# Reordering the state part of a fused Mamba and expert-FFN kernel: B copied first, state product and state step moved forward

## The chip, the cores and the metric

The kernel runs on one core of a Trainium2 chip. The metric is the device time of one execution in microseconds (us), the median of several runs. The engines are named as in the profile: PE (TensorE; PEld is its weight load), DVE (VectorE), ACT (ScalarE), POOL (GpSimd) and SP (SyncE, which here only issues DMAs).

## The reference, cut to what matters

The input x is 8 sequences of 1024 tokens by 256 features. One layer is a mixer with a residual, then a feed-forward part with a residual:

```python
x = x + layernorm(u + mamba(rmsnorm(u)))      # u = layernorm(x)
x = x + layernorm(ffn(layernorm(x)))          # dense MLP + 1024 experts, top 8 of 64x(16..64) keys, 4 heads
```

The mixer works in chunks of 128 tokens, with 8 heads of 64 features and a state of 128 per head. In one chunk, after a projection, a causal convolution over 4 taps and a silu:

```python
scores  = (C @ B.T) * decay * dt              # within the chunk
Y_intra = scores @ X
S       = (B * w).T @ X                       # what the chunk adds to the state
Y_inter = (C * exp(cum)) @ H                  # what the state before gives to the chunk
H       = exp(cum_last) * H + S               # the state step
y = rmsnorm((Y_intra + Y_inter + D*X) * silu(z)) @ out_w
```

## The kernel before, in words

Work is cut into 32 groups of 256 tokens, and a group into two chunks c = 0, 1. Each engine runs its own instruction list, written out by hand in a function `do_group(g, e, f, n)`; a hardware loop runs it once per period. In one period four groups are in flight: group g is in the mixer, e = g-1 in the first half of the feed-forward part, f = g-2 in its last part, and n = g+1 only has its input normalised. Engines execute their lists strictly in order, and semaphores order them against each other (`X.at(g, k)` is the count that says step k of group g is done). So the order of calls in each engine's `do_group` is the schedule.

PSUM is eight banks: `ring[0:2]` (the projection's pairs, X transposed, the state products), `pairb[0:2]` (decay rows, B transposed, scores, y transposed, the output), `yb` (hT, cum, the intra-chunk output), `f0` (the feed-forward output) and `products` (two banks, the expert products).

First part of a period. PE computes ten pairs of projection tiles (`mixer_pair`, L1340) into `ring`, with the feed-forward matmuls of e and f between them. ACT takes the halo and begins each pair (`mixer_pair`, L685 and L694), DVE adds three taps (`mixer_conv`, L998 and L1008), ACT applies silu (L675). DVE's top-8 search `ffn_best(e, c)` (L1097 on) stands between conv(6), conv(7) and conv(8, 9).

Second part, the state part. PE, in this order: `mixer_X(g, 0)` (L1391), the transposes of W (L1534), the expert products (L1504), the decay rows (`mixer_rows`, L1376 and L1379), `ffn_out(f, 1)` (L1554), `mixer_hT(n)` (L1309), B transposed (`mixer_B`, L1400), scores (L1423), the inter-chunk product `mixer_Yi` (L1413), the intra-chunk product `mixer_Yn` (L1448 and L1452), then for chunk 1 X and rows, the state product of chunk 0 `mixer_S` (L1432), B, scores, Yi, Yn, y transposed (`mixer_yT`, L1461), `mixer_S` of chunk 1, and the output matmuls (`mixer_out`, L1471). The next period's first pair (L1340) stands right behind.

ACT copies what PE transposes: `mixer_B` is `Btok` (L741), which scores waits for; `mixer_hT` is L659, `mixer_move` is `Xt` (L734), `mixer_decay` is `Ldec` (L723, four instructions of a half), `ffn_out` is `f` (L843). `mixer_square(g, c)` (L757) squares the gated y for the norm and waits for DVE's `mixer_gate(g, c)`. DVE multiplies scores by decay (`mixer_scores`, `sL`, L1024), scales Yi by exp(cum) (`mixer_state`, L1034), adds Yn and gates by z (`mixer_gate`, L1045 and L1048), adds S to H (`mixer_step`, L1040), and between these works through the experts of e (`ffn_last` L1159, `ffn_mask` L1168, `ffn_times` L1177) and stores f (`ffn_store`, L1191 and L1195). The period ends on DVE with `tail_sum` (L1059), which waits for the output matmuls. POOL scales X (L467, L473, L493), builds the expert scores (`weigh`, L535), scales the state (`mixer_decay`, L484), and makes the small roots (L508 and L510, `rsf`).

Of the kernel before, what the change touches and what calls it, by code (L numbers as in the profile page):

```python
# [73 lines left out]
def sandwich(nc, x, in_wT, norm_w, conv_w, conv_b, dt_bias, A_log, D_skip, gnorm_w, out_wT,  # L74
# [21 lines left out]
    with ExitStack() as ctx:  # L96
# [227 lines left out]
        def _(pool):  # L324
# [233 lines left out]
            def do_group(g, e, f, n):  # L558
                a, b, c = g is not None, e is not None, f is not None
                if a:  # L560
                    mixer_dt_abs(g)
                if b:
                    tail_root4(e)
                if c:
                    collect(f, 0, 2, 3)
                if a:
                    mixer_dt(g)
                    mixer_keep(g)
                if c:
                    collect(f, 1, 1, 2, 3)  # L570
                if a:
                    mixer_cum(g)
                if n is not None:
                    mixer_norm(n)
                    mixer_halo(n)
                if a:
                    mixer_scale(g, 0)
                    mixer_skip(g, 0)
                if b:
                    weigh(e, 0, 0, 1, 2, 3)  # L580
                if a:
                    mixer_decay(g, 0)
                if c:
                    tail_root(f, statsf, mvf, vf, rsf, rootf)
                if a:
                    mixer_scale(g, 1)
                    mixer_skip(g, 1)
                    mixer_decay(g, 1)
                if b:
                    weigh(e, 1, 0, 1)  # L590
                if a:
                    mixer_root_y(g)
                if b:
                    collect(e, 0, 1)
                if a:
                    tail_root(g, stats3, mv2, ve3, rs3, root3)
                if b:
                    weigh(e, 1, 2, 3)
                pool.wait_ge(own_pool, own.n)
                pool.sem_clear(own_pool)  # L600
                own.restart()
# [14 lines left out]
        def _(act):  # L616
# [228 lines left out]
            def do_group(g, e, f, n):  # L845
                a, b, c = g is not None, e is not None, f is not None

                def pairs(*js):

                    for j in js:  # L850
                        if a:
                            if j >= 2:
                                silu(g, j - 2)
                            mixer_pair(g, j)

                pairs(0, 1)
                if a:
                    mixer_dt(g)
                pairs(2)
                if a:  # L860
                    mixer_u(g)
                if b:
                    tail_norm(e, g)
                pairs(3)
                if b:
                    tail_h2T(e)
                if a:
                    mixer_dt_exp(g)
                    mixer_z(g, 0)
                    mixer_z(g, 1)  # L870
                if b:
                    ffn_sim(e, 0)
                if c:
                    ffn_experts(f, 1, 0)
                pairs(4)
                if b:
                    ffn_sim(e, 1)
                if c:
                    ffn_experts(f, 1, 1)
                pairs(5)  # L880
                if c:
                    ffn_experts(f, 1, 2)
                if b:
                    ffn_up(e, 0)
                if c:
                    ffn_WT(f, 0)
                pairs(6)
                if c:
                    ffn_experts(f, 1, 3)
                if b:  # L890
                    ffn_up(e, 1)
                pairs(7)
                if a:
                    mixer_cum(g)
                pairs(8)
                if b:
                    ffn_up(e, 2)
                pairs(9)
                if b:
                    ffn_up(e, 3)  # L900
                if a:
                    silu(g, PAIRS - 2)
                    silu(g, PAIRS - 1)
                    mixer_move(g, 0)
                if c:
                    ffn_WT(f, 1)
                if b:
                    ffn_exp(e)
                if a:
                    mixer_exp(g)  # L910
                    mixer_decay(g, 0)
                if n is not None:
                    mixer_norm(n, e)
                    mixer_hT(n)
                if c:
                    ffn_out(f)
                if a:
                    mixer_B(g, 0)
                if a:
                    mixer_move(g, 1)  # L920
                    mixer_decay(g, 1)
                    mixer_square(g, 0)
                    mixer_B(g, 1)
                if b:
                    tail_keep(e)
                    ffn_experts(e, 0, 0, 1)
                if a:
                    mixer_yT(g, 0)
                    mixer_square(g, 1)
                    mixer_yT(g, 1)  # L930
                if b:
                    ffn_experts(e, 0, 2)
                if b:
                    ffn_experts(e, 0, 3)
# [14 lines left out]
        def _(dve):  # L949
# [87 lines left out]
            def mixer_step(g, c):  # L1037
                dve.wait_ge(H_scaled.sem, H_scaled.at(g, c))
                dve.wait_ge(S_ps.sem, S_ps.at(g, c))
                V.tensor_tensor(H[:], H[:], ring[c][:], ALU.add).then_inc(H_done.sem, 1)  # L1040
# [156 lines left out]
            def do_group(g, e, f, n):  # L1197
                a, b, c = g is not None, e is not None, f is not None

                def conv(*js):  # L1200
                    for j in js:
                        if a:
                            mixer_conv(g, j)

                conv(0)
                if b:
                    tail_residual(e)
                conv(1)
                if c:
                    ffn_last(f, 1)  # L1210
                    ffn_mask(f, 1, 0)
                conv(2, 3)
                if c:
                    ffn_times(f, 1, 0)
                    for h in range(1, RH):
                        ffn_mask(f, 1, h)
                        ffn_times(f, 1, h)
                conv(4, 5, 6)
                if b:
                    ffn_best(e, 0)  # L1220
                conv(7)
                if b:
                    ffn_best(e, 1)
                conv(8, 9)
                if n is not None:
                    mixer_stats(n)
                if b:
                    ffn_choose(e)
                if c:
                    ffn_stats(f)  # L1230
                if a:
                    mixer_scores(g, 0)
                    mixer_state(g, 0)
                if b:
                    ffn_last(e, 0)
                    ffn_mask(e, 0, 0)
                if c:
                    ffn_store(f)
                if a:
                    mixer_gate(g, 0)  # L1240
                    mixer_step(g, 0)
                if b:
                    ffn_times(e, 0, 0)
                    ffn_mask(e, 0, 1)
                if a:
                    mixer_scores(g, 1)
                if b:
                    ffn_times(e, 0, 1)
                if a:
                    mixer_state(g, 1)  # L1250
                if b:
                    ffn_mask(e, 0, 2)
                if a:
                    mixer_gate(g, 1)
                if b:
                    ffn_times(e, 0, 2)
                if a:
                    mixer_step(g, 1)
                if b:
                    ffn_mask(e, 0, 3)  # L1260
                    ffn_times(e, 0, 3)
                if a:
                    tail_sum(g)
                dve.wait_ge(own_dve, own.n)
                dve.sem_clear(own_dve)
                own.restart()
# [19 lines left out]
        def _(pe):  # L1286
# [271 lines left out]
            def do_group(g, e, f, n):  # L1558
# [54 lines left out]
                    mixer_rows(g, 0, f)  # L1613
                if c:
                    ffn_out(f, 1)
                if n is not None:
                    mixer_hT(n, e)
                if a:
                    mixer_B(g, 0)
                    mixer_scores(g, 0)  # L1620
                    mixer_Yi(g, 0)
                    mixer_Yn(g, 0, e, n)
                    mixer_X(g, 1)
                    mixer_rows(g, 1, f)
                    mixer_S(g, 0)
                    mixer_B(g, 1)
                    mixer_scores(g, 1)
                    mixer_Yi(g, 1)
# [66 lines left out]
```

## Time and profile before

| what | us |
|---|---|
| median of 3 runs | 3009.18 |
| lowest and highest | 2999.34 and 3031.3 |
| the profiled execution's own time | 3042.37 |
| its span, first to last instruction | 3040.6 |
| PE busy | 2806.7 (92%) |
| DVE busy | 2522.2 (83%) |
| POOL busy | 2016.2 (66%) |
| ACT busy | 1722.3 (57%) |
| mean granted TensorE clock | 0.963 |

The last row says what share of full speed the chip granted to PE, averaged over the span; 1.00 is 2.4 GHz and 0.50 is 1.2 GHz. Times of day in the rows are us from the span's start. A group of instructions in the trace carries its count (x16), the time from its first start to its last end, and in brackets the idle time of its engine before it, with what ended it.

### The profile page before, as it was taken

Reading aid. Unit: us, or ns where it says so; the run is one execution under the profiler, and the core shown is the slowest. Engines: PE = TensorE matmul, PEld = TensorE weight load, DVE = VectorE, ACT = ScalarE, POOL = GpSimd, SP = SyncE. Lnnn points to the kernel's source line nnn. Section 1 sums busy time; section 2 is a strip of 40 time slices with the busy share of each in tenths; the row PEclk is TensorE's granted clock in tenths of the full one; section 3 lists DMA queues with packets and bytes.
Section 4 is the critical chain, followed back from the end, with each engine's and each line's share of the span. In section 5 each row is a group of like instructions: output and inputs, shape, how many; then the busy total and the mean of one; then the engine's idle time right before and its main releaser. Section 6 shows DMA issues by size and latency. Waiting matters only on the chain.

```text
span 3040.6 us, 50162 instructions
## 1 busy us (share of the span) xinstructions
PE 2806.7 (92%) x14784; PEld 2295.6 (75%) x14784; DVE 2522.2 (83%) x6406; ACT 1722.3 (57%) x3560; POOL 2016.2 (66%) x2388
## 2 busy tenths in 40 slices
PE   5899999999999999999999999999999999999985
PEld 4777777777777777877777777777777777777763
DVE  4588888888888888888888888888888888888874
ACT  4465556655665655556655565555566555556542
POOL 3287667676677676667676667676667676676755
PEclk9999999999999999999999999999999999999997
DMA  3000000000000000000000000000000000000000
GB/s 124 8 8 11 8 7 7 10 10 10 7 7 10 7 10 10 10 3 7 10 10 10 3 10 7 10 10 10 3 10 7 10 10 10 3 10 7 8 4 7
DMA packets 28183, 34.24 MB, mean 11 GB/s; under 512 B 2672, under 2 KB 27248, under 8 KB 27440
## 3 DMA queue, kind: packets, MB, share of 16 engines
q1 hardware_dynamic: 28144, 33.77, 3.4%
q8 instruction: 19, 0.31, 0.0%
q14 instruction: 20, 0.16, 0.0%
HBM read 25.37 MB, written 8.39 MB: 11 GB/s over the span
## 4 chain that ended last, share of the span: by engine, by line
PE 43%; DVE 23%; ACT 13%; POOL 10%; issue 9%; ACTq 1%; DMA 0%; DVEq 0%; SPq 0%; POOLq 0%
DVE acc L1008 9%; PE bank L1340 8%; POOL Em L535 7%; PE bank L1546 7%; PE bank L1471 4%; PE bank L1359 4%; PE products L1504 4%; PE bank L1423 3%; PE bank L1413 3%; ACT Em L824 2%; ACT WT L834 2%; DVE s L1097 2%; PE bank L1452 2%; PE bank L1495 2%; PE bank L1432 2%
## 5 line engine op out<-in xcount | busy, mean ns | idle before, releaser
L1008 DVE SCALAR_TENSOR_TENSOR acc<-bank,cw,acc 128x253 f32<-128x253 f32 (+2 forms) x1920 | 774.3, 473 | 0.0
L1340 PE MATMUL bank<-hT,w_in 128*128 128x256 f32 x2560 | 608.5, 383 | 11.6 <-DVE acc L1008 10.9
L1340 PEld LDWEIGHTS bank<-hT,w_in 128*128 128x128 f32 x2560 | 485.0, 192 | 117.8 <-issue 44.4
L535 POOL TENSOR_TENSOR Em<-ee 128x1024 f32<-128x1024 f32 x256 | 519.4, 2054 | 28.7 <-issue 28.7
L1168 DVE SCALAR_TENSOR_TENSOR Em<-Em,p 128x1024 f32<-128x1024 f32 x256 | 371.5, 1451 | 0.0
L550 POOL TENSOR_TENSOR W<-W,Em 128x1024 f32<-128x1024 f32 x128 | 335.9, 2624 | 8.6 <-ACT Em L824 0.3
L824 ACT ACTIVATE Em<-Em,rden 128x1024 f32<-128x1024 f32 x256 | 292.5, 1143 | 64.6 <-DVE Em L1177 63.0
L694 ACT ACTIVATE acc<-bank,cb,cw 128x256 f32<-128x256 f32 x640 | 325.2, 561 | 0.0
L1177 DVE TENSOR_TENSOR Em<-Em,products 128x1024 f32<-128x1024 f32 x256 | 311.0, 1215 | 4.5
L675 ACT ACTIVATE xbcT<-acc 128x512 f32<-128x512 f32 x320 | 200.6, 627 | 102.5 <-DVE acc L1008 102.2
L1504 PE MATMUL products<-w_de,h2T 128*128 128x512 f32 x512 | 235.4, 603 | 23.0 <-DVE Em L1177 23.0
L1423 PE MATMUL bank<-xbcT 128*128 128x128 f32 x1024 | 161.1, 322 | 100.5 <-ACT Btok L741 100.5
L1519 PE MATMUL bank<-h2T,w_up 128*128 128x256 f32 x1024 | 242.2, 380 | 1.4 <-ACT sim L796 0.7
L1554 PE MATMUL bank<-w_ue,WT 128*128 128x256 f32 x1024 | 233.8, 382 | 2.1 <-ACT WT L834 2.1
L359 POOL TENSOR_SCALAR ve<-mv 128x2 f32<-128x2 f32 x32 | 9.0, 280 | 341.0 <-DVE mv L976 341.0
L1546 PE MATMUL bank<-w_down,hid 128*128 128x256 f32 x1024 | 233.8, 382 | 0.0
L1423 PEld LDWEIGHTS bank<-xbcT 128*128 128x128 f32 x1024 | 146.2, 228 | 115.7 <-ACT Btok L741 115.7
L1519 PEld LDWEIGHTS bank<-h2T,w_up 128*128 128x128 f32 x1024 | 194.7, 190 | 28.6 <-ACT sim L796 1.5
L1546 PEld LDWEIGHTS bank<-w_down,hid 128*128 128x128 f32 x1024 | 194.2, 192 | 28.6 <-issue 0.7
L1554 PEld LDWEIGHTS bank<-w_ue,WT 128*128 128x128 f32 x1024 | 193.8, 192 | 28.1 <-ACT WT L834 2.5
L685 ACT ACTIVATE halo<-bank 128x6 f32<-128x6 f32 x320 | 56.0, 175 | 273.2 <-PE bank L1340 273.1
L484 POOL TENSOR_TENSOR H<-H,ecum 128x512 f32<-128x512 f32 x64 | 66.7, 1042 | 201.6 <-PE bank L1413 201.6
(177 smaller groups left out, 5799.8 us busy)
## 6 DMA issues: line engine op xcount, KB each, us to landing
x_in<-x_dram SPq DMA_DIRECT2D x32, 256.0 KB, 2.7
x_res<-x_dram SPq DMA_DIRECT2D x32, 256.0 KB, 2.6
out_dram<-f SPq DMA_DIRECT2D x32, 256.0 KB, 2.2
w_in<-in_wT_dram SPq DMA_DIRECT2D x1, 3080.0 KB, 13.0
w_up<-upT_dram SPq DMA_DIRECT2D x1, 1024.0 KB, 15.7
w_de<-down_eT_dram SPq DMA_DIRECT2D x1, 1024.0 KB, 17.7
w_down<-downT_dram SPq DMA_DIRECT2D x1, 1024.0 KB, 19.7
w_ue<-up_e_dram SPq DMA_DIRECT2D x1, 1024.0 KB, 21.8
```

The source lines that it names most:

```text
L535: nc.gpsimd.tensor_tensor(Em[:, k], bc(ee[:, k, 0:XD], 2, KEYS), bc(ee[:, k, XD:XD + KEYS], 1, XD), ALU.mult).then_inc(E_done.sem, 1)
L550: nc.gpsimd.tensor_tensor(W[:], flat[0] if h == 1 else W[:], flat[h], ALU.add)\
L694: last = nc.scalar.activation(acc[:, r, a], ps[:, a * TOK:(a + 1) * TOK], ACT.Identity, scale=cw[:, t, TAPS - 1:TAPS], bias=cb[:, t:t + 1])
L824: nc.scalar.activation(flat, flat, ACT.Silu, scale=rden[:, c, h:h + 1]).then_inc(Zs_done.sem, 1)
L1008: ins = V.scalar_tensor_tensor(acc[:, r, a, ahead:], ps[:, a * TOK:(a + 1) * TOK - ahead], cw[:, t, k:k + 1], acc[:, r, a, ahead:], ALU.mu ...
L1168: V.scalar_tensor_tensor(flat, flat, p8[:, k, TOP - 1:TOP], flat, ALU.is_ge, ALU.mult)\
L1340: last = mm(ring[j % 2][:, a * TOK:(a + 1) * TOK], w_in[:, k, at:at + P], hT[:, k, :], start=k == 0, stop=k == DK - 1)
L1423: last = mm(pairb[q][:, i * P:(i + 1) * P], xbcT[:, INNER // P + h, c * P:(c + 1) * P], xbcT[:, INNER // P + HEADS + h, c * P:(c + 1) * P] ...
L1504: last = mm(fA[:, q * 512:(q + 1) * 512], h2T[:, k, c * P:(c + 1) * P], w_de[:, k, q * 512:(q + 1) * 512], start=k == 0, stop=k == DK - 1)
L1519: last = mm(yb[:, a * TOK:(a + 1) * TOK], w_up[:, k, (2 * j + a) * P:(2 * j + a + 1) * P], h2T[:, k, :], start=k == 0, stop=k == DK - 1)
L1546: last = mm(f0[:, c * D:(c + 1) * D], hid[:, i, c * P:(c + 1) * P], w_down[:, i, :], start=False, stop=False)
L1554: last = mm(f0[:, c * D:(c + 1) * D], WT[:, 4 * q + i, :], w_ue[:, 4 * q + i, :], start=False, stop=c == CH - 1 and q == 1 and i == 3)
```

## The change

Only the order of calls changes, on all four compute engines. POOL scales the state (`mixer_decay(g, 0)`) after the first expert head instead of after the fourth. ACT copies B of chunk 0 ahead of `ffn_out` and `mixer_hT`, and B of chunk 1 ahead of the square. DVE runs conv(8) ahead of the second `ffn_best`, `mixer_state` ahead of `mixer_scores`, and `mixer_step` ahead of `ffn_store` and `mixer_gate`. PE runs B and Yi of chunk 0 ahead of `mixer_hT`, and S ahead of Yn.

```diff
 POOL
-                    weigh(e, 0, 0, 1, 2, 3)
+                    weigh(e, 0, 0)
                 if a:
                     mixer_decay(g, 0)
+                if b:
+                    weigh(e, 0, 1, 2, 3)
 ACT
                     mixer_norm(n, e)
+                if a:
+                    mixer_B(g, 0)
+                if c:
+                    ffn_out(f)
+                if n is not None:
                     mixer_hT(n)
-                if c:
-                    ffn_out(f)
-                if a:
-                    mixer_B(g, 0)
                 if a:
                     mixer_move(g, 1)
                     mixer_decay(g, 1)
+                    mixer_B(g, 1)
                     mixer_square(g, 0)
-                    mixer_B(g, 1)
 DVE
-                conv(7)
+                conv(7, 8)
                 if b:
                     ffn_best(e, 1)
-                conv(8, 9)
+                conv(9)
...
                 if a:
+                    mixer_state(g, 0)
                     mixer_scores(g, 0)
-                    mixer_state(g, 0)
                 if b:
                     ffn_last(e, 0)
                     ffn_mask(e, 0, 0)
+                if a:
+                    mixer_step(g, 0)
                 if c:
                     ffn_store(f)
                 if a:
                     mixer_gate(g, 0)
-                    mixer_step(g, 0)
 PE
+                if a:
+                    mixer_B(g, 0)
+                    mixer_Yi(g, 0)
                 if n is not None:
                     mixer_hT(n, e)
                 if a:
-                    mixer_B(g, 0)
                     mixer_scores(g, 0)
-                    mixer_Yi(g, 0)
+                    mixer_S(g, 0)
                     mixer_Yn(g, 0, e, n)
                     mixer_X(g, 1)
                     mixer_rows(g, 1, f)
-                    mixer_S(g, 0)
                     mixer_B(g, 1)
```

## Rows read from the trace of the kernel before

**Rows 1.** The page: PE's share of the span, and the chain that ended last.

```profile
PE 2806.7 (92%) x14784; PEld 2295.6 (75%) x14784; DVE 2522.2 (83%) x6406; ACT 1722.3 (57%) x3560; POOL 2016.2 (66%) x2388
...
PE 43%; DVE 23%; ACT 13%; POOL 10%; issue 9%; ACTq 1%; DMA 0%; DVEq 0%; SPq 0%; POOLq 0%
```

**Rows 2.** Stretches of one period: length, busy PE PEld DVE ACT POOL, clock, DMA, GB/s.

```profile
913.53:1002.63 89.10, 84.31 (x463) 68.97 (x462) 77.93 (x200) 53.53 (x111) 63.34 (x75) 1.00 0.03 9
1278.01:1371.56 93.55, 88.77 (x463) 72.86 (x462) 78.97 (x201) 52.82 (x111) 63.07 (x75) 0.95 0.03 8
```

**Rows 3.** Timeline of DVE: L1059 of the third and of the last period.

```profile
275.71 0.88 DVE L1059 SCALAR_TENSOR_TENSOR v<-bank,rsy,u 128x256 f32<-128x256 f32 x2 [1.20 <-PE bank L1471]
...
2934.70 0.88 DVE L1059 SCALAR_TENSOR_TENSOR v<-bank,rsy,u 128x256 f32<-128x256 f32 x2 [1.56 <-PE bank L1471]
```

**Rows 4.** Timeline of PE, state part of one period at full clock.

```profile
966.64 0.38 PE L1376 MATMUL bank<-mask_b,ident_b 128*128 128x512 bf16 x1
...
974.57 2.05 PE L1423 MATMUL bank<-xbcT 128*128 128x128 f32 x16 [0.79 <-ACT Btok L741]
...
980.84 0.61 PE L1391 MATMUL bank<-ident,xbcT 128*128 128x128 f32 x4
...
983.49 1.90 PE L1432 MATMUL bank<-Xw,Btok 128*128 128x64 f32 x16
...
988.86 2.05 PE L1423 MATMUL bank<-xbcT 128*128 128x128 f32 x16 [2.59 <-ACT Btok L741]
990.75 1.90 PE L1413 MATMUL bank<-H,xbcT 128*128 128x64 f32 x16
...
993.39 1.89 PE L1452 MATMUL bank<-Xdt,sL 128*128 128x64 f32 x16
...
1000.46 1.97 PE L1471 MATMUL bank<-w_out,yT 128*128 128x256 f32 x8 [0.78 <-ACT yT L765]
1002.26 3.62 PE L1340 MATMUL bank<-hT,w_in 128*128 128x256 f32 x16
```

**Rows 5.** Timeline of PE, the same product in a period with a lower clock.

```profile
1172.68 3.52 PE L1413 MATMUL bank<-H,xbcT 128*128 128x64 f32 x16
```

**Rows 6.** Stretches of that period: PE waiting, then PE behind the wait.

```profile
1167.80:1170.20 2.40, 0.00 (x0) 0.00 (x0) 2.37 (x4) 1.24 (x4) 2.02 (x2) 1.00 0.30 109
...
1172.00:1178.00 6.00, 6.00 (x25) 4.97 (x23) 4.04 (x5) 3.02 (x5) 1.64 (x2) 0.50 0.00 0
```

**Rows 7.** Timeline of DVE in the full-clock period.

```profile
956.10 1.11 DVE L1097 MAX8 s<-sim 128x8 f32<-128x64 f32 x8
...
980.96 2.06 DVE L1168 SCALAR_TENSOR_TENSOR Em<-Em,p 128x1024 f32<-128x1024 f32 x1
983.94 1.45 DVE L1191 TENSOR_SCALAR f<-f,mvf,rsf 128x256 f32<-128x256 f32 x2 [0.92 <-POOL rsf L510]
...
987.49 0.67 DVE L1040 TENSOR_TENSOR H<-H,bank 128x512 f32<-128x512 f32 x1
...
989.22 1.27 DVE L1168 SCALAR_TENSOR_TENSOR Em<-Em,p 128x1024 f32<-128x1024 f32 x1
990.41 1.28 DVE L1024 TENSOR_TENSOR sL<-bank,Ldec 128x512 f32<-128x512 f32 x2
...
995.40 0.69 DVE L1045 TENSOR_TENSOR yv<-yv,bank 128x512 f32<-128x512 f32 x1 [0.46 <-PE bank L1452]
...
1000.21 1.22 DVE L1177 TENSOR_TENSOR Em<-Em,products 128x1024 f32<-128x1024 f32 x1
```

**Rows 8.** Timeline of ACT in the full-clock period.

```profile
956.14 1.01 ACT L694 ACTIVATE acc<-bank,cb,cw 128x256 f32<-128x256 f32 x2
...
982.59 2.25 ACT L723 ACTIVATE Ldec<-bank,ncum 128x128 f32<-128x128 f32 x8 [0.51 <-PE bank L1379]
...
988.23 1.06 ACT L741 ACTIVATE Btok<-bank 128x512 f32<-128x512 f32 x2
```

**Rows 9.** Timeline of POOL in the full-clock period.

```profile
992.82 1.04 POOL L484 TENSOR_TENSOR H<-H,ecum 128x512 f32<-128x512 f32 x1 [4.35 <-PE bank L1413]
```

More of the change, by code:

```diff
@@ L913, in do_group @@
                     mixer_norm(n, e)
-                    mixer_hT(n)
+                if a:
+                    mixer_B(g, 0)
                 if c:
                     ffn_out(f)
-                if a:
-                    mixer_B(g, 0)
+                if n is not None:
+                    mixer_hT(n)
                 if a:
```

## The prediction

> **What bounds the kernel now.** I read the page first. PE is busy for 92% of the span, DVE for 83%, and the chain that ended last lies on PE for 43%, on DVE for 23%, on ACT for 13% and on POOL for 10% [rows 1]. So no engine alone sets the time: a period starts with a PE-bound stretch, and then a chain that crosses all four engines decides when the output matmuls are done and the next period's first pair may start.
>
> Next I measured the period, from one L1059 to the next. From the third to the last there are 29 periods in 2934.70 - 275.71 = 2658.99 us [rows 3], a mean of 91.69. But single periods differ: 89.10 at a granted clock of 1.00, 93.55 at 0.95 [rows 2]. Three periods in a row, ending with the one shown, are the 89.1 kind. The work is the same, so this trace holds its own experiment: 29 x 89.10 = 2583.9, and the remaining 75.1 us, 2.6 per period, are what the lower clock costs. The stretches of one slowed period show where it happens: PE does nothing for 2.40 us at clock 1.00, and from 1172 to 1178 it is granted 0.50, which is 1.2 GHz instead of 2.4 [rows 6]; the inter-chunk product takes 3.52 us there against 1.90 at full clock [rows 4, 5]. What PE did before the fall is wait for Btok, 2.59 us in the period shown [rows 4]. That longest wait of the period does not bring the fall every time (this very period kept its clock), but falls come after it.
>
> Why that wait: ACT copies B of chunk 1 behind the square of chunk 0, at 988.23 [rows 8], the square waits for DVE's gate, the gate for the store of f, and the store for POOL's rsf (0.92 idle ahead of it) [rows 7].
>
> **The change part by part**, on the full-clock period. Nothing is added or removed; no DMA moves.
>
> *conv(8) ahead of the second top-8 search.* DVE is free at 956.10 [rows 7], but ACT has only just begun pair 8: L694 starts at 956.14 and takes 1.01 [rows 8]. Today the search fills this time. With the new order DVE idles about 1.05 us plus a hand-over that I estimate at 0.15 from the other places where conv waits for ACT: 1.2 us. Conv(9) ends 1.2 later, so do the silu, X's copy, WT's copy, the exponentials, the expert choice, POOL's four expert heads, rsf, and the store. PE gains nothing from the earlier conv(8): its products then end sooner, and it waits for WT's copy instead, so that the decay rows start some 0.46 later than 966.64 [rows 4] (1.2 less 0.75 of slack between that copy's first half and the rows). Bounds: 0, if DVE arrives late anyway, and 1.4, if the hand-over is twice as long. I take +1.2 on the DVE and POOL chain.
>
> *B and Yi of chunk 0 first, hT and ffn_out behind.* This fills the 0.79 wait for Btok at 974.57 [rows 4]: 1.7 us of Yi stand in it. The copies of f and hT come about 1 us later on ACT, which waits afterwards anyway for X of chunk 1. f's statistics are then ready near 976, and POOL wants them only near 983. Cost 0.
>
> *S ahead of Yn.* PE's S at 983.49 takes 1.90 from first start to last end, of which some 0.16 lies under the next operation: 1.74 [rows 4]. It moves in front of X of chunk 1, which then starts at 980.84 + 0.46 - 0.79 + 1.74 = 982.25. Rows follow, and Ldec starts 982.59 + 1.4 = 984.0 and ends at 986.25 [rows 8]. Formerly S hid the wait for Ldec; now PE waits about 1.2 us there in three pieces (under each half of B, and for the first half of Btok).
>
> *POOL's state decay after one head, DVE's step ahead of the store.* Four heads plus decay take POOL the same time in either order; Yi is ready near 975.6 and POOL asks near 976.5, so nothing stalls. DVE has its step ready near 982.4, behind the mask, and waits for rsf until 985.1 (983.9 + 1.2): the step is free there, and its 0.67, or 0.60 without what overlaps its neighbour, leaves the tight part [rows 7]. mixer_state ahead of scores likewise uses time in which DVE waits: 0.
>
> *B of chunk 1 copied ahead of the square.* Btok starts at 986.25, behind Ldec, instead of 988.23 [rows 8]. Scores start near 986.9 instead of 988.86, Yi ends near 990.2 instead of 992.48. Now sL is late: DVE reaches it at 990.41 + 1.2 - 0.6 = 991.0 and has it at 992.3 [rows 7]. The intra-chunk product starts at 992.4 instead of 993.39 [rows 4], so 0.99 earlier, after a wait of about 1.2. From there PE's list is unchanged down to the next first pair: 1002.26 - 1.0 = 1001.3. The gate no longer waits its 0.46 [rows 7].
>
> *Sum.* DVE's last product ends at 1000.21 + 1.22 + 1.2 - 0.6 - 0.46 = 1001.6; PE's outputs arrive at about the same time (formerly DVE waited 1.20 there) [rows 3]. So both chains give 1.0 us less, a full-clock period of 88.1. DVE is the bound of the second half then.
>
> *The clock.* PE's longest wait, 2.59, is split: 1.2 in three pieces around B, 1.2 ahead of Yn. In before, the other waits of 0.79 and 0.78 [rows 4] are followed by no fall. I take it that the falls go. Lower bound of this gain 0, upper 75.1 us. The Trainium skill (TensorE: Matmul & The Clock Gate, What's actually happening) says that the clock is gated by how busy PE has recently been; the halved clock behind PE's wait agrees [rows 6]. Leaving that page out changes no number here.
>
> Price of overlap: the mask takes 1.27 with POOL quiet (989.22) and 2.06 beside POOL's heads (980.96) [rows 7]. POOL's second decay moves from 992.82 [rows 9] to about 990.5, with two more heads behind it, so more of DVE's tight part lies beside POOL. Between 0 and 0.8 per period; I take 0.1, as the operations beside it are mostly the same in number. The Trainium skill (SBUF — State Buffer, Who interferes with whom) has an exclusive lock here for a DVE instruction with two SBUF inputs against POOL's reads. By its rule a mask caught behind a head could wait much of it; the rows show 0.79 more.
>
> Total: 2583.9 + 75.1 goes to 29 x 88.1 = 2554.9, that is -104; two more periods ahead of them at -1 each, and 0.1 x 31 back: about -103. The profiled execution's own 3042.4 becomes 2939. The median of before is 33 lower than this execution, presumably with fewer falls; a kernel with no falls should not share in that, so I leave 2939.
>
> **The rivals.**
> *A. The clock keeps falling as before,* 2.6 per period: the waits of 1.2 and 1.2 lie within 7 us, with transposes and short products between them. For it: the fall isn't strictly tied to the long wait. Against: the total idle near it falls from 2.6 to 1.2 at B. Time 2939 + 75 = 3014, no change against the median.
> *B. Slower: the stall ahead of conv(8) is passed through whole.* The DVE and POOL chain from conv(9) to the gate is the true bound, PE's earlier start only waits for it, and the clock still falls. Price 1.2 x 31 = 37: 3042 + 37 = 3079. It is slower by over 1% from 3039 on, so if the step and the gate's wait give back under 1.1 per period and the clock nothing. For it: rsf is waited for in every period. Against: 0.60 and 0.46 are plainly in the rows.
> *C. The stall costs nothing,* because DVE comes late to conv(8) anyway, behind a later tail_sum: then 31 x 1.2 less, 2902.
> *D. It doesn't do what it says:* Btok still comes late, since the Ldec ahead of it is slower or the second half of B waits. Then the clock falls in some periods: 2939 + 35 = 2975.
>
> **How the numbers follow.** The forecast has 0.60 (2915 to 2965), C 0.08, D 0.12, A 0.14, B 0.06. About 1% is what a measurement of this kernel can tell from no change: faster below 2979, slower above 3039. Faster: 0.60 + 0.08 + most of D, with a part of A: 0.79. Slower 0.06, same 0.15. The range goes from C to A, 2895 to 3012.
>
> **What the profile after would show.** Right: periods near 88, clock 1.00 in nearly all, Btok of chunk 1 ahead of the square, no PE wait over 1.5 us, L998 of pair 8 waiting about 1.2 for ACT, and L1452 waiting for sL (DVE) in chunk 1; the step ahead of the store with the wait for rsf shrunk. Wrong: stretches at 0.50 in the state part (A), or an Ldec that ends over 1 us later than 986.25 relative to its period (D), or periods over 91 at clock 1.00 (B).

## The result, and the profile after

The changed kernel takes 3118.38 us (median of 4, 3114.32 to 3120.07), against 3019.44 for the kernel before (median of 4: the three runs above and one more): a ratio of 1.0318, with a 95% interval of 1.0263 to 1.0372. It is slower. The forecast was 2939 with a range from 2895 to 3012, so both the direction and the range were wrong. The profiled execution has a span of 3118.3. Each later experiment had the kernel before measured beside it, at 3023.66, 3028.17 or 3029.76, and its ratio is to that; so differences of a few us between experiments mean nothing.

Three lines of the page of the changed kernel; its line numbers are up to 4 above those of before:

```profile
span 3118.3 us, 50134 instructions
...
PE 2865.9 (92%) x14784; PEld 2337.5 (75%) x14784; DVE 2581.2 (83%) x6406; ACT 1724.7 (55%) x3560; POOL 1965.3 (63%) x2388
...
PE 63%; DVE 16%; POOL 9%; issue 7%; ACT 4%; DMA 0%; DVEq 0%; ACTq 0%; SPq 0%; POOLq 0%
```

The same instructions are busy 59 us longer on PE and 59 us longer on DVE than before, and PE's share of the chain rose from 43% [rows 1] to 63%. The engines do no more work, they do it more slowly. Stretches of the changed kernel (length, busy time of PE, PEld, DVE, ACT, POOL, granted clock, DMA): two periods, then two pieces of the second one.

```profile
1135.02:1228.19 93.17, 87.81 (x463) 71.85 (x462) 80.67 (x200) 53.67 (x111) 61.32 (x74) 0.96 0.03 8
1228.19:1323.01 94.82, 89.47 (x463) 73.18 (x462) 79.86 (x200) 53.59 (x111) 61.32 (x74) 0.95 0.03 8
1306.10:1308.70 2.60, 0.00 (x0) 0.00 (x0) 2.60 (x4) 2.57 (x5) 2.60 (x2) 1.00 0.00 0
1310.00:1317.00 7.00, 7.00 (x33) 6.82 (x33) 5.35 (x7) 2.24 (x4) 3.51 (x4) 0.50 0.00 0
```

These answer to [rows 2] and [rows 6]. No period of the loop keeps full clock any more. Before, 3 of the 29 did. Over the 29 periods the granted clock stood at 0.50 for 270 us, and before for 167. PE still waits in one piece, 2.6 us, and its clock is still 1.2 GHz behind it; only the place is new. PE's timeline in that period, against [rows 4]:

```profile
1281.89 0.39 PE L1380 MATMUL bank<-mask_b,ident_b 128*128 128x512 bf16 x1 [1.27 <-ACT WT L836]
...
1290.62 1.95 PE L1427 MATMUL bank<-xbcT 128*128 128x128 f32 x16
...
1303.22 1.90 PE L1417 MATMUL bank<-H,xbcT 128*128 128x64 f32 x16
1304.95 1.08 PE L1452 MATMUL bank<-DX,ident 128*128 128x512 f32 x2
1308.76 3.21 PE L1456 MATMUL bank<-Xdt,sL 128*128 128x64 f32 x16 [2.73 <-DVE sL L1027]
...
1312.61 3.52 PE L1436 MATMUL bank<-Xw,Btok 128*128 128x64 f32 x16
1315.91 3.71 PE L1475 MATMUL bank<-w_out,yT 128*128 128x256 f32 x8
...
1322.64 3.62 PE L1344 MATMUL bank<-hT,w_in 128*128 128x256 f32 x16
```

```profile
1300.66 0.62 ACT L743 ACTIVATE Btok<-bank 128x512 f32<-128x512 f32 x1
```

The wait for Btok in chunk 0 is gone, and B's copy for chunk 1 (the ACT row) and the second Yi come early, as forecast. Then PE waits 2.73 for sL, where I had 1.2, and the intra-chunk product, S and the output matmuls run at half speed (3.71 for the output against 1.97 in [rows 4]). Why sL is late stands on DVE and POOL, side by side in time:

```profile
1271.93 0.35 DVE L1001 SCALAR_TENSOR_TENSOR acc<-bank,cw,halo_sum 128x3 f32<-128x3 f32 x2 [1.07 <-ACT acc L696]
...
1296.92 0.68 DVE L1043 TENSOR_TENSOR H<-H,bank 128x512 f32<-128x512 f32 x1
1299.90 2.25 DVE L1194 TENSOR_SCALAR f<-f,mvf,rsf 128x256 f32<-128x256 f32 x2 [2.31 <-POOL rsf L510]
1302.19 1.41 DVE L1198 TENSOR_TENSOR f<-f,x_late 128x512 f32<-128x512 f32 x1
...
1305.97 1.43 DVE L1171 SCALAR_TENSOR_TENSOR Em<-Em,p 128x1024 f32<-128x1024 f32 x1
1307.33 1.27 DVE L1027 TENSOR_TENSOR sL<-bank,Ldec 128x512 f32<-128x512 f32 x2
```

```profile
1299.84 1.04 POOL L467 TENSOR_TENSOR Xdt<-Xt,dts 128x512 f32<-128x512 f32 x1
1300.96 1.04 POOL L473 TENSOR_TENSOR Xw<-Xdt,ecum 128x512 f32<-128x512 f32 x1
1301.96 1.09 POOL L493 TENSOR_TENSOR DX<-Xt,head_c 128x512 f32<-128x512 f32 x1
```

The store of f took 1.45 in its first part before [rows 7] and 0.69 in its second (L1195, 22.2 us over 32 in its group). It now takes 2.25 + 1.41, together 1.5 more. Beside it POOL runs three operations back to back. Before, the second of them waited for S of chunk 0 (23.8 us in 32 waits), which PE computed late; S is early now, so this gap in POOL's list is gone, and with it the room in which DVE worked undisturbed.

The chain that ended last shows it piece by piece. Rows are start, length and what was running; "issue" is a wait for nothing that the profile shows:

```profile
1299.90 0.03 DVE f L1194
1299.94 1.01 issue
1300.95 1.21 DVE f L1194
1302.19 0.03 DVE f L1198
1302.22 0.09 issue
1302.33 1.20 issue
1303.53 0.69 DVE yv L1048
```

The second half of L1194 gets going at 1300.95, when POOL's first operation has ended (1299.84 + 1.04 = 1300.88). Until then DVE's first half is on record as running, for 1.13 us; but it took 1.13 before the change as well, since POOL's first operation lay beside it there too. New are the second half of L1194, 1.20 instead of 0.40, with POOL's second operation beside it, and L1198, 1.41 instead of 0.69, beside the third.

### The profile page after: what moved, and what is told of

It reads as the page before. It is cut to its first block, busy times and chain, and to the rows that moved or that the text cites. A ratio compares the mean times of both kernels' runs of the same rounds, so it can differ in the third digit from the quotient of the medians.

```text
span 3118.3 us, 50134 instructions
## 1 busy us (share of the span) xinstructions
PE 2865.9 (92%) x14784; PEld 2337.5 (75%) x14784; DVE 2581.2 (83%) x6406; ACT 1724.7 (55%) x3560; POOL 1965.3 (63%) x2388
## 4 chain that ended last, share of the span: by engine, by line
PE 63%; DVE 16%; POOL 9%; issue 7%; ACT 4%; DMA 0%; DVEq 0%; ACTq 0%; SPq 0%; POOLq 0%
PE bank L1344 16%; PE bank L1558 7%; PE bank L1550 7%; POOL Em L535 7%; PE bank L1475 5%; DVE acc L1011 5%; PE bank L1523 4%; PE bank L1363 4%; PE products L1508 4%; PE bank L1499 4%; PE bank L1436 3%; PE bank L1456 3%; PE bank L1383 2%; DVE Em L1171 2%; DVE Em L1180 1%
## 5 line engine op out<-in xcount | busy, mean ns | idle before, releaser
L535 POOL TENSOR_TENSOR Em<-ee 128x1024 f32<-128x1024 f32 x256 | 544.0, 2145 | 28.5 <-issue 28.5
L1171 DVE SCALAR_TENSOR_TENSOR Em<-Em,p 128x1024 f32<-128x1024 f32 x256 | 448.5, 1752 | 0.0
L1456 PEld LDWEIGHTS bank<-Xdt,sL 128*128 128x128 f32 x1024 | 141.3, 217 | 122.0 <-issue 122.0
L1456 PE MATMUL bank<-Xdt,sL 128*128 128x64 f32 x1024 | 144.0, 302 | 81.8 <-DVE sL L1027 81.8
L1001 DVE SCALAR_TENSOR_TENSOR acc<-bank,cw,halo_sum 128x3 f32<-128x3 f32 x640 | 109.5, 212 | 119.4 <-ACT acc L696 119.3
```

The costliest lines, as they stand in the source:

```text
L535: nc.gpsimd.tensor_tensor(Em[:, k], bc(ee[:, k, 0:XD], 2, KEYS), bc(ee[:, k, XD:XD + KEYS], 1, XD), ALU.mult).then_inc(E_done.sem, 1)
L1171: V.scalar_tensor_tensor(flat, flat, p8[:, k, TOP - 1:TOP], flat, ALU.is_ge, ALU.mult)\
L1456: last = mm(yb[:, h * HD:(h + 1) * HD], sL[:, h, :], Xdt[:, h * HD:(h + 1) * HD], start=False, stop=h == HEADS - 1)
```

## The experiments

Two things are suspected, the granted clock and the store of f, and the parts of the change may differ in sign. A kernel that keeps PE busy in its wait measures the order alone, at full clock.

**PE kept busy in its wait, both orders.** The same addition in both; in the old order ahead of the second scores, in the new one ahead of the intra-chunk product of chunk 1:

```diff
+            def warm(f, count):
+                if f is not None:
+                    pe.wait_ge(f_sb.sem, f_sb.at(f))
+                    for _ in range(count):
+                        mm(f0[:], zero_b[:], mask_b[:].rearrange("p h t -> p (h t)"), start=True, stop=True)
...
                     mixer_B(g, 1)
+                    warm(f, 11)
                     mixer_scores(g, 1)
```

Old order:

> The order of before, with eleven 128x512 bf16 matmuls of zeros on PE (some 2.4 us) in its 2.59 us wait ahead of the scores of chunk 1; they go to the bank f0, which holds nothing then, and change no result. Theory 1 (the clock falls because PE has been idle there): no stretch at 0.50 is left in the loop and every period takes 89.1 to 89.4 us, so the profiled execution comes to 3040 - 75 = 2965 (2955 to 2985). Theory 2 (the falls have another cause, the short products around the wait for instance): the mean period stays near 91.5 and the time near 3020.

New order:

> The changed kernel, with eleven such matmuls in the 2.73 us wait for sL ahead of the intra-chunk product of chunk 1. Theory 1 (most of the 2.6 us per period that the change cost is the clock, which now stays at 0.50 longer and over dense output matmuls): periods near 90.0 at clock 1.00, and 3118 - 31 x 3.9 = 2997 (2980 to 3015), still some 25 above the old order treated alike, since DVE reaches sL 1.6 us later than I forecast. Theory 2 (the new order is slow by itself, and the clock is beside the point): over 3060. Theory 3 (my forecast of the order was right at full clock): periods of 88.1, 2940.

Measured: 2960.68 (ratio to before 0.9817, 0.9734 to 0.9901) and 2985.78 (0.9897, 0.9867 to 0.9928). One period of each:

```profile
1251.86:1340.86 89.00, 86.38 (x469) 69.87 (x472) 77.83 (x201) 53.52 (x111) 63.23 (x75) 1.00 0.03 9
```

```profile
1355.32:1445.20 89.88, 86.52 (x470) 69.89 (x473) 79.04 (x201) 53.71 (x112) 62.24 (x75) 1.00 0.03 9
```

Work that computes nothing makes both kernels faster: the falls come from PE's idleness in those waits. It also divides the result, roughly, since the medians of before alone lie 10 us apart. At full clock the new order costs 2985.8 - 2960.7 = 25 us. The clock costs the old order 3019.4 - 2960.7 = 59 us, and the new one 3118.4 - 2985.8 = 133, which is about half of its 270 us at 0.50. Of the 99 us by which the change is slower, some 74 are the clock.

**Conv(8) alone, and taken back.**

```diff
-                conv(7)
+                conv(7, 8)
                 if b:
                     ffn_best(e, 1)
-                conv(8, 9)
+                conv(9)
```

> The order of before with conv(8) ahead of the second top-8 search and nothing else. If the stall of 1.2 us that this puts on DVE is passed through whole: 3019 + 31 x 1.2 = 3056. If it is absorbed, because PE's wait for Btok is longer or the clock's falls differ: 3019 to 3030. If the clock's falls grow with the longer wait ahead of the scores: up to 3100.

> The changed kernel with conv(8) behind the second top-8 search again. The DVE chain to sL of chunk 1 is then 1.2 us shorter and PE's wait ahead of the intra-chunk product near 1.5 us. If the falls come from that wait: hardly any are left, and the period is 89 us, 2960 to 2990. If only the 1.2 us come back: 3118 - 37 = 3081. If contention of POOL and DVE in the state part is all that matters: 3100 and more.

> The order of before with only conv(8) moved, and sixteen matmuls of zeros (3.5 us) in PE's wait for Btok of chunk 1, which is 3.76 in that order. If the 132 us that conv(8) alone cost are 1.2 us of stall per period and the rest the clock: periods of 90.3 at clock 1.00, 2961 + 37 = 2998 (2990 to 3006). If the move costs more by itself: 3020 and more. If nothing but the clock: 2961.

Conv(8) alone: 3155.32 (1.0459, 1.0369 to 1.0549), with one other the dearest of all. Its price is not the 37 us of the stall but 132. PE's wait for Btok grew from 2.59 to 3.76, and the products behind it are slow:

```profile
1314.59 3.78 PE L1423 MATMUL bank<-xbcT 128*128 128x128 f32 x16 [3.76 <-ACT Btok L741]
1318.16 3.51 PE L1413 MATMUL bank<-H,xbcT 128*128 128x64 f32 x16
```

With PE kept busy it takes 3027.62 (1.0022, 0.9994 to 1.0050), 67 above the old order treated alike (2960.7) instead of the 37 expected: a mean period of 91.1 against 89.05, which is 2.0 more, not 1.2. So about half of the 132 is the later chain itself, and the other half the clock. The missing part stands in the store of f again, whose second operation had taken 0.69:

```profile
1444.10 1.45 DVE L1191 TENSOR_SCALAR f<-f,mvf,rsf 128x256 f32<-128x256 f32 x2 [0.92 <-POOL rsf L510]
1445.58 1.54 DVE L1195 TENSOR_TENSOR f<-f,x_late 128x512 f32<-128x512 f32 x1
```

Here DVE comes later relative to PE's S, POOL's gap is smaller (it waited 0.46 for S), and Xw runs beside the second operation. Taking conv(8) back from the changed kernel gives 3087.30 (1.0252, 1.0157 to 1.0347), 31 less. My third alternative was 3100 and more, my second 3081; it lies at the second. PE's wait for sL stays 2.73 in 24 of 29 periods, since both of its sides come earlier, and the clock falls in 27 of 29. Its two periods without a fall take 88.8, so even at full clock conv(8) cost about 1 us of each period.

**The other parts alone.** S, decay and step early:

```diff
-                    weigh(e, 0, 0, 1, 2, 3)
+                    weigh(e, 0, 0)
                 if a:
                     mixer_decay(g, 0)
+                if b:
+                    weigh(e, 0, 1, 2, 3)
...
+                    mixer_S(g, 0)
                     mixer_Yn(g, 0, e, n)
                     mixer_X(g, 1)
                     mixer_rows(g, 1, f)
-                    mixer_S(g, 0)
...
+                if a:
+                    mixer_step(g, 0)
                 if c:
                     ffn_store(f)
                 if a:
                     mixer_gate(g, 0)
-                    mixer_step(g, 0)
```

> The order of before with S of chunk 0 ahead of the intra-chunk product, POOL's decay after one head and DVE's step ahead of the store, nothing else. S no longer keeps POOL waiting, so the store of f is stretched by 1.5 us as in the changed kernel, the square and the Btok behind it come later, and PE's wait for Btok grows from 2.59 to about 3.5. Theory 1 (longer wait, longer falls): three windows at half clock per period, a period of 94 to 96, 3100 to 3160. Theory 2 (the step early gives back what the stretch takes, and the clock doesn't follow the wait): 3020 to 3050.

Measured 3157.34 (1.0443, 1.0393 to 1.0492). The size fits the first theory, but its mechanism doesn't. PE waits 6.27 for Btok, not 3.5, and the falls are hardly longer: 198 us at 0.50 over the 29 periods against 167 before, worth some 15 us, while the mean period grew from 91.69 to 95.55, which is 112 us over the same 29. The rest is the wait itself. The longest of this kernel's waits tells where it comes from:

```profile
POOL H L484 <- PE bank L1416: 373.9, 64, 9.4
```

POOL waits for Yi 64 times, twice per group, and 373.9 us in all; before it was 201.6 in 33. Without the chunk 0 part Yi comes late, POOL stands still after its first head, and rsf comes 3.3 us later in its period. In the changed kernel, which has that part, POOL waits for Yi only 75.2 us in 34 waits. So this part needs the next one.

Chunk 0 alone (B and Yi ahead of hT on PE, B's copy first on ACT, state first on DVE; PE's part is shown):

```diff
+                    mixer_B(g, 0)
+                    mixer_Yi(g, 0)
                     mixer_hT(n, e)
-                    mixer_B(g, 0)
                     mixer_scores(g, 0)
-                    mixer_Yi(g, 0)
```

> The order of before with only the chunk 0 part: B and the inter-chunk product ahead of hT, state ahead of scores. It takes 0.79 us off PE's wait ahead of the first scores, but nothing off the chain through POOL and DVE that ends in the square and in Btok of chunk 1. Theory 1 (what PE gains it waits for later, in one piece, and the clock falls for longer): the wait for Btok is about 3.4, periods are 92.5 to 95, 3060 to 3130. Theory 2 (the time of PE's earlier start is kept): 3019 - 31 x 0.8 = 2995. Theory 3 (neutral, and the clock doesn't follow): 3019.

Measured 3052.63 (1.0091, 1.0062 to 1.0121), against 3028.17 of before. PE's earlier start is not kept, as the first theory says, but the clock does not fall for longer: it stands at 0.50 for 113 us over the 29 periods, against 167 before. What makes this kernel slower is, by its rows, the store of f, which is stretched here too. S comes early, POOL no longer waits for it, and the store's operations take 1153 ns (mean of its first two) and 1366, against 792 and 693: 1.4 us more per period. With PE's earlier start this also makes PE's wait longer than the 3.4 that I gave:

```profile
1368.07 3.60 PE L1424 MATMUL bank<-xbcT 128*128 128x128 f32 x16 [4.96 <-ACT Btok L741]
```

A wait of 4.96 with a mean clock of 0.971, and one of 3.76 with 0.944 in the kernel with conv(8) alone: the length of the wait alone does not give the length of the fall.

B of chunk 1 ahead of the square, alone:

```diff
                     mixer_decay(g, 1)
+                    mixer_B(g, 1)
                     mixer_square(g, 0)
-                    mixer_B(g, 1)
```

> The order of before with one exchange: ACT copies B of chunk 1 ahead of the square of chunk 0. PE's 2.59 us wait for Btok goes, and sL (DVE, 1.6 us later) leaves a wait of some 0.3 to 1.0 ahead of the intra-chunk product. Theory 1 (falls follow the long wait): no falls, a period of 87.6 to 88.2, and 2910 to 2935, under both kernels. Theory 2 (the order of the state part has falls whatever its waits): 2975 to 3010.

Measured 2930.03 (0.9682, 0.9635 to 0.9729), as the first theory has it. This exchange is worth 98 us by itself, of which 2960.7 - 2930.0 = 31 would be there at full clock too, and it is one of the changed kernel's. PE's waits are short (0.51 for sL here, 0.63 or 0.64 in the other 28 periods), and no period of the loop has a fall:

```profile
1318.44 2.05 PE L1423 MATMUL bank<-xbcT 128*128 128x128 f32 x16 [0.25 <-ACT Btok L741]
...
1323.65 1.97 PE L1452 MATMUL bank<-Xdt,sL 128*128 128x64 f32 x16 [0.51 <-DVE sL L1024]
```

**POOL held until f is stored.** This is the test of the stretched store:

```diff
                     tail_root(f, statsf, mvf, vf, rsf, rootf)
+                    if a:
+                        pool.wait_ge(o_done.sem, o_done.at(f))
                 if a:
                     mixer_scale(g, 1)
```

It goes into the changed kernel:

> The changed kernel; before POOL scales X of chunk 1 it waits until DVE has stored f. In the changed kernel DVE's store took 2.25 + 1.41 us beside these three POOL operations, against 1.45 + 0.69 before. Theory 1 (the store is stretched by POOL's operations, this makes sL late, and the wait of PE ahead of the intra-chunk product, now 2.73, brings the falls): the store is back at 1.5 + 0.7, the wait shrinks to 1.3 to 1.8, few or no falls are left, the period goes to 88.5 to 89.5 and the time to 2940 to 2980. Theory 2 (the falls come from something other than that wait, and only the stretch itself is gained): 3118 - 31 x 1.3 = 3078. Theory 3 (the stretch has another cause): 3110 to 3130.

Measured 3013.73 (0.9959, 0.9935 to 0.9983). One added wait takes 105 us off and the loss against before is gone. The store is even shorter than before the change, 0.74 + 0.69:

```profile
1343.05 0.74 DVE L1196 TENSOR_SCALAR f<-f,mvf,rsf 128x256 f32<-128x256 f32 x2 [2.31 <-POOL rsf L510]
1343.83 0.69 DVE L1200 TENSOR_TENSOR f<-f,x_late 128x512 f32<-128x512 f32 x1
```

Its cause is shown by that: the same DVE operations, with only POOL's order against them changed. But it is not as fast as I expected, since the clock still falls in 16 of the 29 periods, right behind a wait of only 1.19. PE's longest wait in this kernel is another one, 1.49 ahead of the decay rows and 25 us earlier, where it waits for WT's copy; conv(8) makes it.

```profile
1439.79 1.97 PE L1458 MATMUL bank<-Xdt,sL 128*128 128x64 f32 x16 [1.19 <-DVE sL L1029]
...
1442.18 3.52 PE L1438 MATMUL bank<-Xw,Btok 128*128 128x64 f32 x16
```

The two kinds of period of this kernel:

```profile
1271.36:1360.46 89.10, 84.83 (x462) 69.20 (x464) 78.70 (x200) 52.51 (x110) 61.16 (x74) 1.00 0.03 9
1360.46:1452.41 91.95, 87.33 (x458) 71.35 (x460) 79.22 (x201) 54.65 (x112) 63.41 (x75) 0.96 0.03 9
```

The first kind shows that the store is not all. At full clock, and with a store shorter than before the change, this order takes 89.10, just what the old one took, and not the 88.1 of the forecast. DVE's list ends the period (no idle time ahead of L1064), and in it the masks are stretched; POOL's decay of chunk 1 and two heads now lie beside them. Before, the two masks around sL took 1.27 (989.22, in [rows 7]) and 1.60:

```profile
993.34 1.60 DVE L1168 SCALAR_TENSOR_TENSOR Em<-Em,p 128x1024 f32<-128x1024 f32 x1
```

In this kernel:

```profile
1347.41 1.93 DVE L1173 SCALAR_TENSOR_TENSOR Em<-Em,p 128x1024 f32<-128x1024 f32 x1
1348.44 1.80 POOL L484 TENSOR_TENSOR H<-H,ecum 128x512 f32<-128x512 f32 x1 [0.18 <-PE bank L1419]
1350.20 3.76 POOL L535 TENSOR_TENSOR Em<-ee 128x1024 f32<-128x1024 f32 x2
1352.19 2.85 DVE L1173 SCALAR_TENSOR_TENSOR Em<-Em,p 128x1024 f32<-128x1024 f32 x1
1360.46 0.87 DVE L1064 SCALAR_TENSOR_TENSOR v<-bank,rsy,u 128x256 f32<-128x256 f32 x2
```

They take 1.93 and 2.85. The mean of all masks, eight per period, is 1770 ns here and 1752 in the changed kernel, against 1451 before.

With conv(8) back as well, and then with five matmuls of zeros more ahead of the intra-chunk product:

> The changed kernel with conv(8) back and with POOL's wait for the store of f. At full clock 89.1 (the period of the kernel with POOL's wait) - 1.1 = 88.0. Theory 1 (falls depend on how long PE waits in one piece): its wait ahead of the intra-chunk product stays 1.2, as both sides of it move together, and falls remain in some periods: 2930 to 2980. Theory 2 (the falls of the kernel with POOL's wait came from the longer wait ahead of the decay rows that conv(8) makes): no falls, 2923.

> The kernel of the run before this one, with five matmuls of zeros in the 1.2 us ahead of the intra-chunk product. All theories: no falls, periods near 88.0, 2918 to 2928. It is the new order without its two costs, and tells what the order itself is worth: 2961 - 2923, 38 us, if the idea behind the steps of my sum is right.

Measured 2925.39 (0.9691, 0.9620 to 0.9762) and 2921.70 (0.9676, 0.9605 to 0.9746). There are no falls without the zeros either. PE's wait for sL is 0.73 to 1.10 there (mostly 0.82), not the 1.2 I gave, and the wait for WT's copy is gone; conv(8) was part of what kept falls alive, and which of the two waits mattered is not separated. Freed of these two costs the new order is 2960.7 - 2921.7 = 39 us faster than the old one at full clock. But not all of that is the order: B of chunk 1 first gives 31 of it alone, and POOL's wait helps the old order too, as the next kernel shows.

**The best found**, the old order with B of chunk 1 first and POOL's wait:

> Only B of chunk 1 ahead of the square, and POOL's wait for the store of f. If the stretch of the store (792 against 460 ns for each half) is on the path that ends in sL, which PE waits 0.51 us for: 88.2 - 0.5 = 87.7 and 2915. If POOL's later X of chunk 1 makes the intra-chunk product wait instead: 2930 to 2960.

Measured 2909.32 (0.9633, 0.9563 to 0.9703): 120 us below before (3029.76 beside it) and 209 below the changed kernel. POOL's wait is worth 2930.0 - 2909.3 = 21 here, 6 more than expected, and the masks take 1429 ns in the mean, the least of all these kernels. The other state parts of the change, which the kernel at 2921.7 has on top of this one, cost 12 us.

```profile
1321.49:1408.86 87.37, 84.40 (x459) 68.76 (x461) 77.93 (x202) 53.70 (x111) 62.55 (x75) 1.00 0.03 9
```

The 29 periods of the loop in the profiled executions, side by side. The last column is how long the granted clock stood at 0.50 in them, read from the clock of each period:

| kernel | median, us | mean period | us at 0.50 |
|---|---|---|---|
| before (profiled at 3042) | 3019 to 3030 | 91.69 | 167 |
| changed | 3118 | 94.21 | 270 |
| changed, conv(8) back | 3087 | 93.36 | 266 |
| changed, POOL waits | 3014 | 90.63 | 109 |
| conv(8) alone | 3155 | 95.46 | 290 |
| S, decay and step early | 3157 | 95.55 | 198 |
| chunk 0 alone | 3053 | 92.16 | 113 |
| all others | 2909 to 3028 | 87.3 to 91.1 | 0 |

## Why the prediction was wrong, step by step

At full clock the changed kernel takes 2985.8 where 2939 was forecast, 47 more, and the clock costs another 133. To compare places in a period I set the first part's last projection pair equal, 957.59 in the full-clock period of before and 1272.26 after: 314.67 apart.

*The stall ahead of conv(8)*: right on DVE, 1.07 idle and sL's chain about 1.2 later. Rsf was put at 985.1 and came at 1299.86 - 314.67 = 985.2. That PE gains nothing and waits for WT's copy is right too (1.27).

*B and Yi first, S early, decay and step early*: the step was to be free near 982.4 and ran at 1296.92 - 314.67 = 982.3. Btok was put at 986.25 and came at 1300.66 - 314.67 = 986.0, and the second Yi was to end near 990.2, and what stands behind it began at 1304.95 - 314.67 = 990.3. This geometry held to 0.3 us.

*Price of overlap* is the first step that failed. I took 0.1 per period, with 0.8 as the upper end, and looked only at the masks beside POOL's heads. At full clock the period came out at 89.9 instead of 88.1, 1.8 more. The store of f lies on the tight path too, and I had said myself that S moves. I didn't follow who waits for S: POOL's Xw of chunk 1 did, and its wait was what kept POOL off DVE during the store. It cost 1.5 us, and sL was ready at 1308.6 - 314.67 = 993.9 and not at 992.3. Nor were the masks rightly sized, the term that I did have: their mean grew by 0.3 us each, eight times per period. With the store unstretched, POOL's wait gave back 0.8 of the 1.8, and the stretched masks are what stands in DVE's list beyond the forecast there; no run removes them alone from this order, so their share is read from the rows and not tested. The page that I named there (SBUF — State Buffer, Who interferes with whom, in the Trainium skill) says that whichever of the two engines issues first has the shared ports for its whole instruction and the other stands still. It says so for a DVE operation in a mode that takes both ports, which a tensor_scalar can enter; that L1194 is in that mode no run here shows. The trace agrees as far as it goes: the first half takes 1.13 us and ends with POOL's operation, against 0.41 with POOL held. I weighed that page against the masks and not against the operations that the change brought together.

*The clock* is the second. "I take it that the falls go" rested on a wait of 1.2 ahead of Yn; it was 2.73. And even the premise was too weak: in the kernel with POOL's wait a wait of 1.19 is followed by falls in half the periods. It also left out the wait for WT's copy, 1.27, which the forecast itself had named ahead of the decay rows. The place of the falls is new but no dearer: a period with 6.8 us at 0.50 takes 3.2 us more than one with none before, and 3.3 more than the 89.9 of full clock in the changed kernel. What grew is the time at 0.50. Rival A had the falls persist at their old price of 2.6 per period; they cost 133 us, 4.3 per period. A's own time of 3014 lay just outside the range that was to reach it.

*The rivals.* Slower, B, had 0.06, and its condition was worked out slightly wrong: from 3079 down to 3039 are 40 us, 1.3 per period and not 1.1. It named the right part, the stall of conv(8), and the clock still falling, for 3079. What it lacked is that a later DVE lengthens PE's wait, that this wait costs clock, and that the store is stretched. Two things that none of my cases had make a shift cost more than itself: a later DVE (conv(8) alone, +132, with 290 us at 0.50 instead of 167), and an earlier S, which ends POOL's wait and stretches the store (chunk 0 alone, +24, with less time at 0.50 than before).

What stays open is what decides whether a short wait brings a fall, and for how long it lasts; the waits here range from 1.19 to 6.27 us, and the loss doesn't follow their order.

## What to carry to other kernels

Where PE waits for another engine in one piece, look at the clock behind the wait before moving anything: a change that makes the other engine later can cost as much again in clock (65 of 132 us here), and filling the wait with work that computes nothing shows at once what the order alone is worth. When an operation is moved earlier, ask whose wait it ends, and what that engine will then run beside; a POOL wait that looks idle may be what lets DVE's store run at its own speed. Test the parts of a reordering one by one: of the four here one is worth 98 us and two cost over 120 alone.

## What the runs showed of the hardware

The same DVE store of f took 0.74 + 0.69 us with POOL held back, 1.45 + 0.69 with POOL partly beside it, and 2.25 + 1.41 with three POOL operations back to back. In one kernel a wait of PE of 1.19 us was followed by a fall to 1.2 GHz in 16 of 29 periods, while waits of 0.51 to 0.64 in another and of 0.73 to 1.10 in a third were followed by none. The length of the wait alone does not tell: 2.6 us brought falls in 26 of 29 periods, and 4.96 us brought 3.4 us at 1.2 GHz in most periods where 3.76 brought 10.2. Matmuls of zeros in bf16 were enough to keep the clock at 2.4 GHz across a wait of 2.6 us.
